# A fused last layer in a one-core attention kernel: part of the output product made ahead, in two other stages

## The chip, the cores and the metric

The kernel runs on one core of one Trainium2 chip. The metric is the device time of one execution in microseconds (us). Its engines here: TensorE (PE; PEld is its weight load), VectorE (DVE), ScalarE (ACT), GpSimd (POOL) and SyncE (SP), which issues DMAs only.

## The reference

x has 128 sequences of 32 rows and 256 features; everything is fp32.

```
x = x + einsum('bct,bcd->bdt', x, w0[subject])        # L0, 32x32 mixing of the rows, by sequence
x = x + einsum('bct,bcd->bdt', x, w1[condition])      # L1, the same
# L2: attention. q (8 heads of 32), k, v (4 heads) = projections of x; rms norm and rope on q, k;
#     the 32 new k, v rows are written into a paged cache (16 positions a block), a window of 128
#     positions is attended; o @ Wo.T is added
x2 = x + L2(x)
# L3: adapters by sequence
out = x2 + x2 @ W.T + scale[a] * (x2 @ A[a].T) @ B[a].T
```

## The kernel before

**Layout.** A tile is four sequences, 128 rows of x; there are 32 tiles, 16 pairs of tiles, and 64 couples (two sequences each, so two couples in a tile). A group is 8 sequences, two tiles, four couples. The stages:

Index and mixing stage, to about 50 us: which cache blocks a window needs, the row and window indices, and the 32x32 mixing matrices of L0 and L1 for all tiles (`mixT`).

Tile stage, about 50 to 157 us. A loop over pairs (`part2`). TensorE: `xT` of the even tile (L1006, x mixed and transposed), `qkv` (L1015, 512 columns), two `qT` transposes of the pair before (L1022), `xT` and `qkv` of the odd tile. ScalarE: squares (L534), a copy of v (L538), x2T out of PSUM (`xT_out`, L524), `keep_x`, a second copy of it to `xres` (L528), square roots, and the copy of v to `stage`. VectorE: sums of squares, norm, rope, `finish` (L759). GpSimd scatters the new k and v of each tile to `new_scratch` in DRAM (L433). `turn_indices` (L994, L999), on whose result VectorE waits before its first sum, stands behind the first two pairs on TensorE. qkv uses four PSUM banks (`psQKV`). After the `xres` copy this tensor holds x2's part before attention, which only the last layer reads.

Gap. When all scatters have landed, GpSimd fetches the patched blocks of groups 0 and 1 (`from_patched`, L446). VectorE makes masks meanwhile (L872 to L881) and adds the identity to W (`w3_plus_one`, L884), so that out = x2 (W + 1) + adapter. TensorE has nothing to do.

Attention stage, from 180 us. For each group GpSimd gathers the cache blocks (`fetch`, L439) and then the patched ones; SP writes the values to DRAM (`values_out`, L331) and reads them back transposed (`values_in`, L343, L345); they are in the list of SP in this order, with the output stores of two tiles (`store`, L324) between `values_out` and `values_in`. TensorE transposes keys four times a group (`unit`, L1071; L1188 for group 0), in the first two periods of the group before. There is a period for each couple c. TensorE's order in it: scores of c+1 (mask L1084, then L1089), values of c-1 (L1128), a unit, [odd: `adapter`, L1146], the transposes of c's probabilities (L1108, L1113), a unit, then [even: `project`, L1139; odd: `final`, L1152 and L1153] of the last tile. ScalarE: [even: `y_out`, L634], `heads_out` (L626), exponentials of c+1 in two halves (L610) with a unit's copy between and one at the end (L601), `probT_out` (L619). VectorE: maxima of c+1 (L890), [odd: `adapt_in`, L916], the copy of the probabilities (L907), reciprocal and scaling of c+1 (L896, L900), [even: `add3`, L911, between its halves]. Every engine works strictly through its own list; scores of c+2 wait until all exponentials of c+1 have read the four score banks (`expd`). Periods 0 to 7 and the last 8 are written out, the others are a loop of 8.

**The last layer** of a tile in the order of its data: `project` (o Wo, transposed, into bank `psZ`), `add3` (x3T = x2T + that), `adapter` (A x3T), `adapt_in` (times the adapter mask and scale, `xam`), `final` (x3 (W + 1) + xam B), `y_out` (PSUM to one of two buffers `ys`, after waiting for the buffer's store of two tiles ago), `store`. `project` of the next tile waits until `y_out` has emptied psZ.

## Time and profile before

| | us |
|---|---|
| runs | 495.17, 490.85, 505.08; median 495.17 |
| the profiled execution | 493.59 |
| its span, first to last instruction | 491.8 |
| PE busy (share) | 381.8 (78%) |
| DVE busy | 345.4 (70%) |
| ACT busy | 264.4 (54%) |
| POOL busy | 107.7 (22%) |
| mean granted TensorE clock | 0.906 |

The profile is one execution. Its times are from the start of the span; the ends of matmuls are modelled, and "[0.71 <-ACT ...]" behind an instruction is the idle time of its engine before it and what ended it. "issue" is time in which the engine waited for nothing that the profile shows. Each fp32 product of the program shows as two instructions (each L1015 below is four for two products).

### The profile page before, as it was taken

To read this page: it belongs to the slowest core of one execution; us is meant where nothing else is said; L and a number is where in the kernel's file an instruction comes from. 1 tells how busy PE (TensorE), PEld (TensorE's weight loads), DVE (VectorE), ACT (ScalarE), POOL (GpSimd) and SP (SyncE) were. 2 spreads that over 40 slices of the span, in tenths; PEclk is the share of its full clock that TensorE was granted. 3 is DMA by queue.
4 is the path that set the end of the run, shared out by engine and by line. 5 is a ranking of instruction groups with operands and counts; after the bars stand their busy time and mean duration, and the time that the engine had idled before them with its cause. 6 is when DMAs were issued, how large, how long until landed. Compare 5 with 4: busy or idle time off the path is not lost.

```text
span 491.8 us, 16903 instructions
## 1 busy us (share of the span) xinstructions
PE 381.8 (78%) x6190; PEld 283.1 (58%) x6190; DVE 345.4 (70%) x1017; ACT 264.4 (54%) x977; POOL 107.7 (22%) x178
## 2 busy tenths in 40 slices
PE   1753788888885027888798899999699999899996
PEld 0333534444442025676676777777577777777785
DVE  6995189999999515747666777777567677777782
ACT  3303556666664015646465766676456666766662
POOL 5300043333334700221112112111211212111000
PEclk9855789999998555989989999999989999999999
DMA  3999123222202266888887777967977666976200
GB/s 111 354 409 412 49 69 107 73 79 72 78 35 81 61 140 175 150 188 178 172 183 180 155 177 167 145 156 160 204 192 160 159 175 149 181 182 147 73 23 24
DMA packets 68867, 73.58 MB, mean 150 GB/s; under 512 B 18190, under 2 KB 65326, under 8 KB 66528
## 3 DMA queue, kind: packets, MB, share of 16 engines
q1 hardware_dynamic: 61968, 39.38, 33.5%
q0 software_dynamic: 6864, 33.72, 24.9%
q8 instruction: 23, 0.38, 0.3%
q14 instruction: 12, 0.10, 0.1%
HBM read 70.83 MB, written 26.21 MB: 197 GB/s over the span
## 4 chain that ended last, share of the span: by engine, by line
PE 48%; DMA 19%; ACT 12%; issue 11%; DVE 7%; SPq 1%; DVEq 1%; ACTq 0%; POOL 0%; POOLq 0%
ACT rope L610 6%; PE probT_bank L1128 6%; DMA kvbuf<-new_scratch,winidx 6%; PE out_bank L1152 5%; PE score_banks L1015 5%; PE score_banks L1089 5%; PE probT_bank L1015 4%; DMA value_scratch<-kvbuf 4%; PE keys_bank L1071 3%; PE score_banks L1084 3%; ACT window L601 3%; PE score_banks L1006 3%; DMA window<-value_scratch 3%; PE out_bank L1139 3%; DMA out<-early 3%
## 5 line engine op out<-in xcount | busy, mean ns | idle before, releaser
L610 ACT ACTIVATE rope<-score_banks,negm 128x176 f32<-128x176 f32 x256 | 101.8, 413 | 4.5 <-DVE negm L890 4.5
L890 DVE TENSOR_REDUCE negm<-score_banks 128x2 f32<-128x352 f32 x128 | 61.1, 519 | 34.6 <-PE score_banks L1089 34.1
L900 DVE TENSOR_SCALAR rope<-rope,rinv 128x176 f32<-128x176 f32 x256 | 70.9, 319 | 4.6
L626 ACT COPY early<-probT_bank 128x128 f32<-128x128 f32 x64 | 17.0, 266 | 88.6 <-PE probT_bank L1128 88.6
L433 POOL DMA_INDIRECT new_scratch<-stage,rowidx x32 | 36.5, 1139 | 106.7 <-DVE stage L759 101.7
L907 DVE COPY rope<-probT_bank 128x512 f32<-128x512 f32 x64 | 44.3, 692 | 18.0 <-PE probT_bank L1108 14.3
L610 ACT ACTIVATION_READ_ACCUMULATOR rope<-score_banks,negm 128x1 f32 x256 | 54.2, 212 | 0.0
L1128 PE MATMUL probT_bank<-rope,window 128*32 128x64 f32 x2048 | 43.7, 226 | 5.5 <-issue 4.7
L601 ACT COPY window<-keys_bank 128x352 f32<-128x352 f32 x60 | 46.8, 780 | 1.5 <-PE keys_bank L1071 1.5
L1071 PE MATMUL keys_bank<-ident,kvbuf 88*128 88x88 f32 x240 | 32.5, 260 | 16.3 <-ACT window L601 14.3
L1128 PEld LDWEIGHTS probT_bank<-rope,window 128*32 128x32 f32 x2048 | 32.8, 112 | 17.7 <-issue 17.7
L446 POOL DMA_INDIRECT kvbuf<-new_scratch,winidx x16 | 17.1, 1070 | 115.0 <-DMA kvbuf<-in_kv,winidx 112.2
L1108 PE MATMUL probT_bank<-ident,rope 128*128 128x128 f32 x256 | 40.8, 283 | 0.1
L1089 PE MATMUL score_banks<-window,rope 32*64 32x48 f32 (+2 forms) x1536 | 39.8, 292 | 0.0
L1084 PE MATMUL score_banks<-maskB,mask 96*128 96x176 bf16 x256 | 31.7, 248 | 7.8 <-ACT rope L610 6.9
L439 POOL DMA_INDIRECT kvbuf<-in_kv,winidx x16 | 17.4, 1087 | 92.0 <-PE keys_bank L1071 70.2
L1071 PEld LDWEIGHTS keys_bank<-ident,kvbuf 88*128 88x128 f32 x240 | 22.0, 145 | 26.6 <-ACT window L601 21.5
L1006 PE MATMUL score_banks<-kvbuf,work 128*128 (+1 forms) x128 | 22.1, 302 | 19.1 <-ACT x2T L524 16.6
L1139 PE MATMUL out_bank<-early,wts 128*128 128x128 f32 x256 | 36.3, 287 | 0.4 <-ACT early L626 0.4
L1006 PEld LDWEIGHTS score_banks<-kvbuf,work 128*128 128x128 f32 x128 | 18.3, 206 | 31.5 <-issue 28.9
L1152 PE MATMUL out_bank<-wts,early 128*128 128x256 f32 x128 | 34.9, 396 | 0.4 <-DVE early L916 0.4
L1139 PEld LDWEIGHTS out_bank<-early,wts 128*128 128x128 f32 x256 | 32.6, 200 | 0.6 <-ACT early L626 0.5
(184 smaller groups left out, 734.6 us busy)
## 6 DMA issues: line engine op xcount, KB each, us to landing
value_scratch<-kvbuf SPq DMA_DIRECT2D x16, 704.0 KB
window<-value_scratch SPq DMA_DIRECT2D x16, 512.0 KB, 11.7
work<-in_x SPq DMA_DIRECT2D x16, 256.0 KB, 2.7
new_scratch<-window SPq DMA_DIRECT2D x2, 2048.0 KB, 12.1
out<-early SPq DMA_DIRECT2D x32, 128.0 KB, 7.1
window<-value_scratch SPq DMA_DIRECT2D x32, 96.0 KB, 8.8
new_scratch<-kvbuf SPq DMA_DIRECT2D x1, 2048.0 KB, 13.4
wts<-in_weights SPq DMA_DIRECT2D x1, 1280.0 KB, 8.6
```

The source lines that it names most:

```text
L601: a.copy(kT[:, par, :, 4 * u:4 * u + 4].rearrange("p r o -> p o r"), psK[:, 0:4 * GR].rearrange("p (o r) -> p o r", o=4)).then_inc(s["unit ...
L610: ins = a.activation(prob[:, par, P_AT[h]:P_AT[h] + KEYS], psS[:, h, 0:KEYS], ACT.Exp, bias=negm[:, par, h:h + 1], accum_out=sums[:, par, ...
L890: v.tensor_reduce(negm[:, par, 2 * half:2 * half + 2], psS[:, 2 * half:2 * half + 2, 0:KEYS], axis=AX_X, op=ALU.max, negate=True).then_inc ...
L900: ins = v.tensor_scalar(prob[:, par, at], prob[:, par, at], rinv[:, par, h:h + 1], None, ALU.mult)
L907: v.tensor_copy(probT[:, par, 0:512], psP[0][:, :]).then_inc(s["pte0"], 1)
L1006: ins = t_.matmul(psT[j][:, P * c:P * c + P], xin[:, slot, P * c:P * c + P], mixT[:, bass.ds(n, 1), :].rearrange("p o d -> p (o d)"), star ...
L1071: ins = t_.transpose(psK[:, o * GR:(o + 1) * GR], kvbuf[0:GR, par, KV * (4 * u + o):KV * (4 * u + o) + P], ident[0:GR, 0:GR])
L1084: t_.matmul(psS[:, g_, 0:KEYS], mask4[:, tile, k % 2, :], maskB[:, g_ % 2].rearrange("p o i -> p (o i)"), start=True, stop=True, skip_grou ...
L1089: return t_.matmul(psS[64 * b:64 * b + 64, g_, n:n + BLOCK * blocks], qs[HD * g_:HD * g_ + HD, tile, P * (k % 2) + 64 * b:P * (k % 2) + 64 ...
L1128: ins = t_.matmul(headsT[HD * g_:HD * g_ + HD, 64 * b:64 * b + 64], vnat[:, (k // CPG) % 2, 2 * (k % CPG) + b, h, V_AT[g_]:V_AT[g_] + HD], ...
L1139: ins = t_.matmul(psZ[:, P * f:P * f + P], woT[:, u, P * f:P * f + P], oT[:, u, :], start=(u == 0), stop=(u == 1))
L1152: t_.matmul(psZ[:, 0:256], x3T[:, P * f:P * f + P], w3T[:, f, :], start=(f == 0), stop=False)
```

## The change

o Wo (W + 1) is linear, so the last layer splits: out = x2 (W + 1) + o [Wo (W + 1)] + (x2 A' + o [Wo A']) masked, times B. Wo (W + 1) and Wo A' are made once on TensorE in the gap (`fused`) and kept in `wo` and `woA`. x2's part of both (`x2_parts`: two products of 256 columns, two of 128) is made for even tiles in the tile stage, after the first qkv of a pair, into bank `psX`, and for odd tiles in the gap, into the four score banks in turn; ScalarE copies it over `xres` and into `xa2` (`x2_out`). So `keep_x` stays for odd tiles only; psX takes a bank from qkv, which now has two and waits for the norm and the v copy of the tile two back (it was four back). In the attention stage `project` gives o's two parts, `adapter` and `add3` are gone, `final` has the product with B alone, `y_out` moves to VectorE in even periods (ahead of the probabilities' copy) and adds `xres`, and `adapt_in` becomes an add of `xa2` and a separate mask step behind the copy. There are four buffers `ys`; SP's list has `values_in` ahead of the stores. `turn_indices` and `w3_plus_one` stand earlier. VectorE's loop has one more round of 8 periods written out. The semaphores and the closing waits follow.

```diff
@@ -139,11 +139,14 @@
         ident = sb("ident", [P, P])
-        work2 = sb("work2", [P, 3072])
+        work = sb("work", [P, 6144])
+        e1, work2 = work[:, 0:3072], work[:, 3072:]
+        xa2 = [work[:, a:a + TILES // 2 * P].rearrange("p (t n) -> p t n", n=P) for a in (3072, 1024)]
...
         w_at = [sum(W_PARTS[:k]) for k in range(len(W_PARTS))]
-        wqkvT, woT, w3T, laT = (wts[:, a:a + n].rearrange("p (c n) -> p c n", c=2) for a, n in zip(w_at[:4], W_PARTS))
+        wqkvT, wo, w3T, laT = (wts[:, a:a + n].rearrange("p (c n) -> p c n", c=2) for a, n in zip(w_at[:4], W_PARTS))
         lbT = wts[:, w_at[4]:]
+        woA = sb("adapted_wo", [P, 2, P])
...
@@ -251,11 +254,9 @@
         rinv = sb("rinv", [P, 2, KVH])
-        e1 = early[:].rearrange("p a b n -> p (a b n)")
-        oT = e1[:, 256:512].rearrange("p (u n) -> p u n", u=2)
-        x3T = e1[:, 512:768]
-        xam = e1[:, 768:896]
-        ys = e1[:, 896:1408].rearrange("p (a n) -> p a n", a=2)
+        oT = e1[:, 0:256].rearrange("p (u n) -> p u n", u=2)
+        xam = e1[:, 256:384]
+        ys = work2[:, 2048:3072].rearrange("p (a n) -> p a n", a=4)
@@ -264,10 +265,11 @@
-        psT, psQKV, psQT = [psS[:, 2], psS[:, 3]], psP + [psS[:, 0], psS[:, 1]], [psK, psZ]
+        psT, psQKV, psQT = [psS[:, 2], psS[:, 3]], psP + psP, [psK, psZ]
+        psX = psS[:, 1]
...
         all_entries = psZ[:, 0:ENT]
-        turned_rows, turned_wins = psS[:, 0, 0:ROWS], psS[:, 1, 0:2 * GROUPS]
+        turned_rows, turned_wins = psS[:, 0, 0:ROWS], psS[:, 0, ROWS:ROWS + 2 * GROUPS]
...
@@ -348,10 +350,10 @@
                 values_out(grp, par)
+                values_in(grp, par, False)
                 if not (isinstance(grp, int) and grp == 2):
-                    store(grp * 2 - 5, 1)
-                store(grp * 2 - 4, 0)
-                values_in(grp, par, False)
+                    store(grp * 2 - 5, 3 - 2 * par)
+                store(grp * 2 - 4, 2 * par)
...
@@ -523,6 +525,11 @@
+            def x2_out(p, n, bank, home):
+                act.wait_ge(s["x2_made"], p + 1)
+                a.copy(xres[:, bass.ds(n, 1), :].rearrange("p t f -> p (t f)"), bank[:, 0:256])
+                a.copy(home.rearrange("p o n -> p (o n)"), bank[:, 256:384]).then_inc(s["x2_kept"], 1)
...
@@ -568,13 +575,15 @@
                 if s1:
+                    wait_from(act, s["x2_made"], i + 2)
...
                 if s1:
-                    for j in range(2):
-                        keep_x(i * 2 + 4 + j, j)
+                    keep_x(i * 2 + 5, 1)
+                if s2:
+                    x2_out(i + 1, i * 2 + 2, psX, xa2[0][:, bass.ds(i + 1, 1), :])
@@ -626,13 +635,6 @@
-            def y_out(m, par):
-
-                act.wait_ge(s["l3"], m + 1)
-                if not (isinstance(m, int) and m < 2):
-                    act.wait_ge(s_out[par], (m - par) * 8)
-                a.copy(ys[:, par, :], psZ[:, 0:256]).then_inc(s["y"], 1)
...
@@ -640,8 +642,6 @@
                 units = k % CPG < 2 and not (known and group >= GROUPS)
-                if par == 0 and not (known and m < 2):
-                    y_out(m - 2, (k // 2) % 2)
@@ -653,6 +653,13 @@
+
+            act.wait_ge(s["fused"], 2)
+            for u in range(2):
+                a.copy(woA[:, u, :], psP[u][:, 256:384])
+                a.copy(wo[:, u, :], psP[u][:, 0:256]).then_inc(s["fused_kept"], 1)
+            for p in range(TILES // 2):
+                x2_out(PAIRS + p, 2 * p + 1, psS[:, p % 4], xa2[1][:, p:p + 1, :])
...
@@ -852,6 +857,11 @@
             v.tensor_copy(winidx[:].rearrange("p k g -> p (k g)"), turned_wins[0:GR]).then_inc(s["winidx"], 1)
+            dve.wait_ge(s["ld_w"], 16)
+            for c in range(2):
+                ins = v.tensor_tensor(w3T[:, c, P * c:P * c + P], w3T[:, c, P * c:P * c + P], ident[:], ALU.add)
+            ins.then_inc(s["w3_plus_one"], 1)
...
@@ -879,10 +889,6 @@
             ch.mark(v.tensor_scalar(admask[:], ad_f[:], pf[:, 2:3], pf[:, 3:4], ALU.is_equal, ALU.mult))
-            dve.wait_ge(s["ld_w"], 16)
-            for c in range(2):
-                ins = v.tensor_tensor(w3T[:, c, P * c:P * c + P], w3T[:, c, P * c:P * c + P], ident[:], ALU.add)
-            ins.then_inc(s["w3_plus_one"], 1)
@@ -906,15 +912,22 @@
-            def add3(m):
+            def y_out(m, q):
+                dve.wait_ge(s["l3"], m + 1)
+                if not (isinstance(m, int) and m < 4):
+                    dve.wait_ge(s_out[q], (m - q) * 4)
+                v.tensor_tensor(ys[:, q, :], xres[:, bass.ds(m, 1), :].rearrange("p o f -> p (o f)"), psZ[:, 0:256],
+                                ALU.add).then_inc(s["y"], 1)
+
+            def adapt_in(m, odd, at):
                 dve.wait_ge(s["wo"], m + 1)
-                v.tensor_tensor(x3T, xres[:, bass.ds(m, 1), :].rearrange("p o f -> p (o f)"), psZ[:, 0:256],
-                                ALU.add).then_inc(s["x3"], 1)
-
-            def adapt_in(m):
-                dve.wait_ge(s["xa"], m + 1)
-                v.tensor_tensor(xam.rearrange("p (b t) -> p b t", b=SPT),
-                                psZ[:, 256:256 + P].rearrange("p (b t) -> p b t", b=SPT),
+                wait_from(dve, s["l3"], m)
+                v.tensor_tensor(xam, psZ[:, 256:256 + P], xa2[odd][:, bass.ds(at, 1), :].rearrange("p o n -> p (o n)"),
+                                ALU.add).then_inc(s["xa_part"], 1)
+
+            def adapt_mask(m):
+                dve.wait_ge(s["xa_part"], m + 1)
+                v.tensor_tensor(xam.rearrange("p (b t) -> p b t", b=SPT), xam.rearrange("p (b t) -> p b t", b=SPT),
@@ -927,17 +940,18 @@
                 if par == 1 and not (known and m < 1):
-                    adapt_in(m - 1)
+                    adapt_in(m - 1, (k // 2 - 1) % 2, o * 2 + (k // 2 - 1) // 2)
+                if par == 0 and not (known and m < 2):
+                    y_out(m - 2, (k // 2 + 2) % 4)
                 probT_out(c, par)
+                if par == 1 and not (known and m < 1):
+                    adapt_mask(m - 1)
                 if not last:
-                    normalise(c + 1, 1 - par, 0)
-                if par == 0 and not (known and m < 1):
-                    add3(m - 1)
-                if not last:
-                    normalise(c + 1, 1 - par, 1)
+                    for half in range(2):
+                        normalise(c + 1, 1 - par, half)
             dve.wait_ge(s["qte"], TILES)
-            dve.wait_ge(s["xcopy"], TILES)
+            dve.wait_ge(s["xcopy"], PAIRS)
@@ -947,15 +961,18 @@
                 normalise(0, 0, half)
-            for k in range(8):
-                period(0, k)
-            with dve.Fori(1, COUPLES // 8 - 1) as o:
+            for o in range(2):
+                for k in range(8):
+                    period(o, k)
+            with dve.Fori(2, COUPLES // 8 - 1) as o:
...
                 period(COUPLES // 8 - 1, k)
-            add3(TILES - 1)
-            adapt_in(TILES - 1)
+            y_out(TILES - 2, 2)
+            adapt_in(TILES - 1, 1, PAIRS - 1)
+            adapt_mask(TILES - 1)
+            y_out(TILES - 1, 3)
@@ -1009,8 +1026,8 @@
                 pe.wait_ge(s["xte"], n + 1)
-                wait_from(pe, s["norm"], n - 3)
-                wait_from(pe, s["vcopy"], n - 3)
+                wait_from(pe, s["norm"], n - 1)
+                wait_from(pe, s["vcopy"], n - 1)
@@ -1022,6 +1039,13 @@
+            def x2_parts(xt, bank):
+                for f in range(2):
+                    t_.matmul(bank[:, 0:256], xt[f], w3T[:, f, :], start=(f == 0), stop=(f == 1))
+                for f in range(2):
+                    ins = t_.matmul(bank[:, 256:384], laT[:, f, :], xt[f], start=(f == 0), stop=(f == 1))
+                ins.then_inc(s["x2_made"], 1)
...
@@ -1030,6 +1054,8 @@
                     qkv(i * 2 + 2, 2 - slot)
+                    wait_from(pe, s["x2_kept"], i + 1)
+                    x2_parts([x2T[:, 0, f, :] for f in range(2)], psX)
@@ -1039,11 +1065,11 @@
             pe.wait_ge(s["mixT"], 2)
+            turn_indices()
...
             pe.wait_ge(s["ld_w"], 16)
+            pe.wait_ge(s["w3_plus_one"], 1)
             part2(-1, 2, True, True, False)
-            turn_indices()
-            pe.wait_ge(s["winidx"], 1)
@@ -1057,7 +1083,18 @@
             pe.wait_ge(s["vcopy"], TILES)
-            pe.wait_ge(s["w3_plus_one"], 1)
+            pe.wait_ge(s["xcopy"], PAIRS)
+
+            for u in range(2):
+                for at, n, w in ((0, 256, w3T), (256, P, laT)):
+                    for f in range(2):
+                        ins = t_.matmul(psP[u][:, at:at + n], wo[:, f, P * u:P * u + P], w[:, f, :], start=(f == 0), stop=(f == 1))
+                ins.then_inc(s["fused"], 1)
+            pe.wait_ge(s["x2_kept"], PAIRS)
+            for p in range(TILES // 2):
+                if p >= 4:
+                    pe.wait_ge(s["x2_kept"], PAIRS + p - 3)
+                x2_parts([xres[:, 2 * p + 1, P * f:P * f + P] for f in range(2)], psS[:, p % 4])
@@ -1134,23 +1171,15 @@
                 wait_from(pe, s["y"], m)
-                for f in range(2):
-                    for u in range(2):
-                        ins = t_.matmul(psZ[:, P * f:P * f + P], woT[:, u, P * f:P * f + P], oT[:, u, :],
-                                        start=(u == 0), stop=(u == 1))
+                for u in range(2):
+                    t_.matmul(psZ[:, 256:256 + P], woA[:, u, :], oT[:, u, :], start=(u == 0), stop=(u == 1))
+                for u in range(2):
+                    ins = t_.matmul(psZ[:, 0:256], oT[:, u, :], wo[:, u, :], start=(u == 0), stop=False, skip_group_check=True)
...
-
-            def adapter(m):
-                pe.wait_ge(s["x3"], m + 1)
-                for f in range(2):
-                    ins = t_.matmul(psZ[:, 256:256 + P], laT[:, f, :], x3T[:, P * f:P * f + P], start=(f == 0), stop=(f == 1))
-                ins.then_inc(s["xa"], 1)
...
                 pe.wait_ge(s["xam"], m + 1)
-                for f in range(2):
-                    t_.matmul(psZ[:, 0:256], x3T[:, P * f:P * f + P], w3T[:, f, :], start=(f == 0), stop=False)
-                t_.matmul(psZ[:, 0:256], xam, lbT, start=False, stop=True).then_inc(s["l3"], 1)
+                t_.matmul(psZ[:, 0:256], xam, lbT, start=False, stop=True, skip_group_check=True).then_inc(s["l3"], 1)
@@ -1165,8 +1194,6 @@
                     unit(group, (k // CPG + 1) % 2, 2 * (k % CPG))
-                if par == 1 and not (known and m < 1):
-                    adapter(m - 1)
@@ -1189,6 +1216,8 @@
             pe.wait_ge(s["first_units"], 2)
+            pe.wait_ge(s["fused_kept"], 2)
+            pe.wait_ge(s["x2_kept"], TILES)
...
@@ -1220,7 +1248,7 @@
     wqkv = _np.concatenate([wq, t("Wk"), wv], axis=0)
-    wo = t("Wo").reshape(FEAT, KVH, 2, HD).transpose(1, 3, 2, 0).reshape(P, -1)
+    wo = t("Wo").reshape(2, P, KVH, 2, HD).transpose(1, 0, 3, 2, 4).reshape(P, -1)
...
```

## Rows read from the trace of the kernel before

**Rows 1.** Windows: stretch and its length, busy time of engines, granted clock, DMA.
```profile
180.00:200.00 20.00, 16.00 (x224) 12.14 (x225) 10.58 (x30) 11.24 (x35) 2.88 (x4) 0.56 0.58 152
400.00:450.00 50.00, 45.87 (x909) 37.59 (x902) 36.19 (x112) 32.60 (x129) 8.69 (x16) 1.00 0.76 170
```

**Rows 2.** Chain of waits in the tile stage: start, length, what.
```profile
123.07 0.71 PE score_banks L1006 x4
...
126.38 1.73 PE score_banks L1015 x4
...
129.22 0.71 PE score_banks L1006 x4
```

**Rows 3.** Chain of waits in the attention stage.
```profile
420.47 0.94 PE out_bank L1139 x8
...
425.20 0.90 PE out_bank L1152 x4
```

**Rows 4.** Chain of waits at the start of the tile stage.
```profile
55.95 1.72 PE probT_bank L1015 x4
...
61.07 3.33 PE score_banks L1015 x4
```

**Rows 5.** Timeline of TensorE, end of the gap: start, length, instruction, idle before.
```profile
180.11 0.82 PE L1188 MATMUL keys_bank<-ident,kvbuf 88*128 88x88 f32 x4 [21.39 <-DMA kvbuf<-new_scratch,winidx]
```

**Rows 6.** Timeline of TensorE, first groups.
```profile
209.39 0.49 PE L1071 MATMUL keys_bank<-ident,kvbuf 88*128 88x88 f32 x4 [2.08 <-DMA kvbuf<-new_scratch,winidx]
...
215.38 0.65 PE L1128 MATMUL probT_bank<-rope,window 128*32 128x64 f32 x32 [0.79 <-DMA window<-value_scratch]
...
229.28 0.64 PE L1128 MATMUL probT_bank<-rope,window 128*32 128x64 f32 x27 [0.98 <-issue]
```

**Rows 7.** Timeline of TensorE, one group and its neighbours.
```profile
412.43 0.47 PE L1084 MATMUL score_banks<-maskB,mask 96*128 96x176 bf16 x4 [0.36 <-ACT rope L610]
...
416.55 0.47 PE L1084 MATMUL score_banks<-maskB,mask 96*128 96x176 bf16 x4
...
419.94 0.52 PE L1071 MATMUL keys_bank<-ident,kvbuf 88*128 88x88 f32 x4 [0.71 <-ACT window L601]
...
421.23 0.47 PE L1084 MATMUL score_banks<-maskB,mask 96*128 96x176 bf16 x4
...
426.37 0.47 PE L1084 MATMUL score_banks<-maskB,mask 96*128 96x176 bf16 x4
...
430.08 0.48 PE L1084 MATMUL score_banks<-maskB,mask 96*128 96x176 bf16 x4 [0.31 <-ACT rope L610]
```

**Rows 8.** Groups of VectorE's instructions, and two of its timeline.
```profile
L872 DVE TENSOR_TENSOR start_bc<-len_f,rem_bc 128x128 f32<-128x128 f32 x1 | 0.3, 284 | 0.0
...
417.66 0.96 DVE L890 TENSOR_REDUCE negm<-score_banks 128x2 f32<-128x352 f32 x2 [0.44 <-PE score_banks L1089]
...
421.56 0.42 DVE L911 TENSOR_TENSOR early<-xres,out_bank 128x256 f32<-128x256 f32 x1 [1.09 <-PE out_bank L1139]
```

**Rows 9.** Timeline of ScalarE and TensorE around 355 us.
```profile
355.18 0.37 ACT L634 COPY early<-out_bank 128x256 f32<-128x256 f32 x1 [5.46 <-DMA out<-early]
...
358.02 0.80 PE L1084 MATMUL score_banks<-maskB,mask 96*128 96x176 bf16 x4
...
363.60 0.47 PE L1084 MATMUL score_banks<-maskB,mask 96*128 96x176 bf16 x4
```

**Rows 10.** Timeline of SP's DMA issues for one group: start, time to issue.
```profile
413.09 0.94 SPq L331 DMA_DIRECT2D value_scratch<-kvbuf  x1
414.34 3.41 SPq L324 DMA_DIRECT2D out<-early  x2
421.48 0.41 SPq L343 DMA_DIRECT2D window<-value_scratch  x1
422.07 3.99 SPq L345 DMA_DIRECT2D window<-value_scratch  x2
```

**Rows 11.** Timeline of TensorE, the last tile.
```profile
484.84 1.16 PE L1139 MATMUL out_bank<-early,wts 128*128 128x128 f32 x8 [0.38 <-ACT early L626]
```

21 lines of the change are left out of this document (9 added, 12 removed).

## The prediction

> **What bounds the kernel now.** I read the stages first (windows), since the change touches three of them. The tile stage (about 60 to 152 us) I read in the chain of waits [rows 2]: a pair of tiles takes 6.15 us from one row at L1006 to the next. TensorE works 5.04 us of that without a break, until the second L1015 ends at 128.11; the other 1.11 us is ScalarE's squares, values and x2T copy. Whatever TensorE gets more there lengthens each pair. Then comes a gap: TensorE stands 21.39 us, from 158.72 on, until group 0's patched cache block lands and L1188 begins at 180.11 [rows 5]. From there 64 couples follow. Their start is paced by transfers: TensorE waits for group 2's keys until 209.39 and for group 1's values until 215.38 [rows 6]. Later the couples pace themselves; TensorE is busy 45.87 of 50 us, VectorE 36.19, ScalarE 32.60 [rows 1]. A row at L1084 opens each period [rows 7]: 4.12 us from the first row to the second (a fourth period of its group), then 4.68, 5.14 and 3.71 (first, second, third): 17.65 us for a group of two tiles. Two ends are seen in them. Before 412.43 and 430.08 TensorE waits for ScalarE's exponentials, so a third period is a loop of scores, maxima and exponentials. The other three have no wait before L1084: TensorE's own queue ends last, and in the first two of a group that queue stands once in the middle, at the second keys transpose, for ScalarE's copy (0.71 us at 419.94).
>
> **The profiled execution** took 493.59 us with 491.8 of span; the 1.8 around it I keep. The median of the runs is 1.6 above it. I sum against 493.59.
>
> **Tile stage.** Each pair gets x2_parts between the first qkv and qT: two products of 256 columns and two of 128. The trace gives each fp32 product as two instructions. Four of 256 columns take 0.90 us in the chain, eight of 128 take 0.94, so four take 0.47 [rows 3]: 1.37 us. From L1015 (1.73 for four of 512 columns, so 0.86 for 256) it is 1.33. I take 1.35. It lies wholly on the path, since ScalarE's squares of the second tile wait for a qkv that starts so much later. Fifteen pairs count (the part of pair -1 falls into the start, below): 15 x 1.35 = 20.2 us. ScalarE loses keep_x of the even tile and gets two copies, the larger like L634's 0.37 [rows 9]; while TensorE works its 5 us, ScalarE has air for them, and they end before the next x2_parts, so that the single bank psX costs nothing. The stricter wait of qkv (two banks, not four) asks for the norm of the tile two back, a pair earlier on VectorE; it gets 1.35 us more air by the longer pair. At the start the index turn (0.7 us) now stands ahead of the first xT and pair -1 has its x2 part: about 0.6 later together, because the turn stood until now in a stretch where TensorE waited anyway. In return the hole before 60.38 shrinks; the qkv at 61.07 ran at the low clock, 3.33 us against 1.72 at 55.95 [rows 4]. If the clock holds, 1.6 comes back; I take half. Stage: **+20.0** (18.5 to 21.5). POOL's scatters follow VectorE, which follows this path, so the last scatter, group 0's block and all its followers shift by as much.
>
> A rule of the Trainium skill would make this half as dear: "TensorE: Matmul & The Clock Gate", section Back-to-back issue gap, gives N / 2.4 + 2.5 ns for a matmul at full clock, 109 ns for 256 columns. By it the part costs some 0.66 us and the stage +10. The rows show 0.43 us for an instruction of 512 fp32 columns and 0.22 for 256 [rows 2, 3], twice the page's figure; I go by the rows.
>
> **Gap,** in before's time (all of it 20.0 later). TensorE is free at about 159.1. The fused weights are four products of 256 and four of 128 columns, 2.7 us, the sixteen odd parts 21.6. It begins at the low clock; the dense start at 50 us had L1015 back at 1.72 by 55.95 [rows 4], some 5 us at half speed, so 2.4 more. ScalarE's copies lie beside, with four banks. That ends at 185.8, 5.7 us after the block's landing, plus 0.5 if code is late. But TensorE then starts warm (the clock granted in 180 to 200 was 0.56 [rows 1]), and the group's transfers go on without it. Walking on from there (transposes 3.3, periods 3.6, 4.2, 4.2, 3.8, 3.6) the sixth scores begin at 208.5; before it was 205.74. Group 2's keys land at 209.4 and group 1's values at 215.4 as before [rows 6], and the overrun drowns in these waits, up to some 1.4 us more of it. I take **+0.5** (0 to +5). The moved w3_plus_one sits in idle time of VectorE.
>
> The Trainium skill, "Runtime: NRT & Kernel Launch", section Instruction fetch mechanics, says that code is streamed in blocks of 256 instructions, mostly hidden. In the trace TensorE stands 0.98 us inside one product loop at 229.28 with nothing to wait for [rows 6]. The gap's 288 instructions would cross one or two blocks: by the page nothing, by that row 1 to 2 us, which is inside the range above.
>
> **Couples, period by period.** Of a tile's projection (0.94), adapter (0.47 to 0.6) and final (0.90 + 0.45 [rows 3]) there remain 0.47 + 0.90 = 1.37 in the even period and 0.45 in the odd one, 0.9 less. But not evenly:
> First of a group: the second keys transpose still starts 3.39 after the period (419.94, it waits for ScalarE), takes 0.52, then 1.40 instead of 0.94: 4.68 becomes 5.14.
> Second: the same transpose at +3.36, 0.52, final 0.45, and the exponentials end about there: 5.14 becomes 4.20.
> Third: the loop's 3.71, but project now waits for VectorE's y_out, which stands behind the maxima. These start 1.11 after the period and last 0.96, y_out 0.42 like L911 [rows 8], so project starts at 2.55 and ends the period at 3.80.
> Fourth: 4.12 was TensorE's queue; with adapter gone and the final short it is the loop, 0.1 below the third's because ScalarE has no keys copy left over: 3.60.
> Sum 16.74 against 17.65, 0.91 a group. From 215 us on 14.5 groups: **-13.2** (-8 to -17). VectorE's mask step is nearest to L872, 128x128 in SBUF, 0.284 [rows 8].
>
> **Stores.** At 355.18 ScalarE's y_out had stood 5.46 us for an output store (two buffers), and heads_out behind it, on which TensorE waits. Some 4.4 of it were lost to TensorE, and the next period, partly at the low clock, took 5.58 (358.02 to 363.60) instead of 4.12 [rows 9]: 5.9 us. With four buffers the wait looks two tiles further back, 17 us, and the store is issued some 9 us later than now. **-5.9** (to 0). Values first: values_in was issued at 421.48, when values_out of 413.09 had landed [rows 10]; the stores were issued inside that wait, so the order by itself gains nothing. It moves their issue behind values_in on SP, ahead of the next values_out. SP was done with values_in at 426.1 and had some 5 us left there.
>
> **Tail.** From 484.84 [rows 11] to the last store's issue at about 489.6 stand project 1.2, add3 0.45, adapter 0.75, adapt_in 0.35, final 1.6 and y_out 0.4. Then they are project 1.6, adapt_in 0.35, mask 0.3, final 0.5 and y_out 0.45: 1.5 less. The last values, behind the shorter final of tile 30, start 0.5 sooner: **-2.0** (-1 to -2.5).
>
> **Sum:** 493.6 + 20.0 + 0.5 - 13.2 - 5.9 - 2.0 = **493.0 us**. With the bounds taken partly together its own range is 486 to 501.
>
> **Rivals.**
> A, all of TensorE's removed work returns: 0.92 x 29 tiles = 27 us instead of 13: 479. For it: 45.87 of 50 us busy [rows 1]. Against: the waits at 419.94, 412.43 and 430.08 [rows 7], which no removed product shortens. 0.12.
> B, slower: VectorE takes TensorE's place. It is busy 36.19 of 50 us [rows 1], 3.19 a period of 4.41, and 3.32 with half a mask step; add3 goes, y_out comes. The shortest periods above are 3.60 and 3.80, and its steps stand in order, so each waits for the transposes, too. If these waits add 0.3 to 0.5, project (behind y_out) and final (behind the mask) come late, each period grows 0.22, a group takes 17.6 and the steady gain is gone: 493.0 + 13.2 = 506. It decides once the mean period is above 4.4. 0.14.
> C, the gap runs cold: x2_parts at 2.7 us each end at 207, 21 us later than above, and 18 of it show: 511. For it, the clock of 0.56 in 180 to 200 [rows 1]; against, that stretch has short bursts, and 50 to 56 us recovered [rows 4]. 0.05. (The Trainium skill's clock page, section Loop structure matters more than you think, says that dense products keep the high clock; by it C is out.)
> D, the buffers don't do what they say: a late store or late values stop an engine as at 355: 499. 0.08, beside 0.61 for the forecast.
>
> **How the numbers follow.** Two per cent (9.9 us) is about what a measurement of this kernel can tell from no change, with runs from 490.85 to 505.08. The range 483 to 506 leaves out A, most of C and the upper half of B, about 0.2. Faster than 485.3: A and a little of the forecast, 0.15. Slower than 505.1: C, over half of B and a little more, 0.16. Within: 0.69.
>
> **What would show it.** In the trace after: rows at L1006 7.5 us apart in the tile stage; L1188 at about 206, long after its block's landing near 200; periods of 5.1, 4.2, 3.8 and 3.6; no engine waiting for a store. VectorE with no idle before the maxima would be B, x2_parts of over 2 us in the gap C. I would be wrong most if a period ends on something that before's waits hid: a late block of keys, or SP, whose round of values_out, wait, values_in and two stores comes to about 15 of 16.7 us.

## The result and the profile after

The changed kernel took **502.61 us** (median of 4 runs, 499.58 to 505.22) where the kernel before took 495.04 (median of 4, 490.85 to 505.08). Executions of one kernel come in a faster and a slower state, and medians here are over all runs, ratios over those of the faster state alone. The ratio is 1.023, 95% interval 1.016 to 1.030: slower by 2.3% (1.6 to 3.0). The forecast was 493.0, no change. The profiled execution after took 500.77, with 498.9 of span against 491.8: 7.1 us more.

The page after: engines (us busy, share, instructions), then the median time to landing of SP's transfers.

```profile
span 498.9 us, 17056 instructions
...
PE 400.6 (80%) x6206; PEld 290.9 (58%) x6206; DVE 348.2 (70%) x1049; ACT 264.5 (53%) x997; POOL 107.8 (22%) x178
...
window<-value_scratch SPq DMA_DIRECT2D x16, 512.0 KB, 12.8
...
out<-work SPq DMA_DIRECT2D x32, 128.0 KB, 7.5
window<-value_scratch SPq DMA_DIRECT2D x32, 96.0 KB, 10.4
```

TensorE has 18.8 us more to do. On the page of the kernel before, the value windows landed after 11.7 and 8.8 us. Line numbers moved: L1006 is now L1023, L1015 is L1032, L1071 is L1108, L1084 is L1121; x2's part is L1044 and L1046, project L1175 and L1177, the final product L1182, y_out L919, the mask L930.

Windows of the kernel after, as [rows 1]; the stretch 200 to 220 holds its first couples:

```profile
180.00:200.00 20.00, 20.00 (x117) 18.30 (x116) 4.48 (x6) 7.48 (x28) 7.55 (x7) 0.93 0.41 92
200.00:220.00 20.00, 15.89 (x186) 12.82 (x184) 8.35 (x23) 12.03 (x41) 2.85 (x4) 0.75 0.62 160
400.00:450.00 50.00, 41.94 (x858) 31.66 (x860) 35.67 (x116) 29.48 (x121) 10.26 (x17) 1.00 0.83 173
```

In 400 to 450 us TensorE works less than before (41.94 us, not 45.87), while the DMA share rose from 0.76 to 0.83: of the work that was taken away a part came back as waiting.

The chain of waits in the tile stage, one pair, as [rows 2]:

```profile
98.64 0.71 PE score_banks L1023 x4
99.34 1.72 PE probT_bank L1032 x4
101.06 0.86 PE score_banks L1044 x4
101.93 0.45 PE score_banks L1046 x4
...
106.09 0.71 PE score_banks L1023 x4
```

A pair takes 7.45 us instead of 6.15, and the 1.31 us of the two new rows is the difference.

TensorE's timeline in the attention stage: the first scores, one group, then late values, as [rows 6, 7]:

```profile
207.01 0.48 PE L1121 MATMUL score_banks<-maskB,mask 96*128 96x176 bf16 x4 [0.84 <-DVE window L958]
...
338.04 0.47 PE L1121 MATMUL score_banks<-maskB,mask 96*128 96x176 bf16 x4
...
341.44 0.52 PE L1108 MATMUL keys_bank<-ident,kvbuf 88*128 88x88 f32 x4 [0.71 <-ACT window L610]
341.80 0.64 PE L1175 MATMUL out_bank<-work,adapted_wo 128*128 128x128 f32 x4
...
343.14 0.47 PE L1121 MATMUL score_banks<-maskB,mask 96*128 96x176 bf16 x4
...
347.43 0.47 PE L1121 MATMUL score_banks<-maskB,mask 96*128 96x176 bf16 x4
...
350.06 0.68 PE L1175 MATMUL out_bank<-work,adapted_wo 128*128 128x128 f32 x4 [0.18 <-DVE work L919]
...
351.45 0.47 PE L1121 MATMUL score_banks<-maskB,mask 96*128 96x176 bf16 x4
...
354.59 0.70 PE L1182 MATMUL out_bank<-wts,work 128*128 128x256 f32 x2 [0.61 <-DVE work L930]
355.13 0.47 PE L1121 MATMUL score_banks<-maskB,mask 96*128 96x176 bf16 x4
...
414.87 0.65 PE L1165 MATMUL probT_bank<-rope,window 128*32 128x64 f32 x32 [1.54 <-DMA window<-value_scratch]
```

The periods of a group are 5.10, 4.29, 4.02 and 3.68: 17.09 against 17.65. Project now waits for VectorE's y_out and the final product for its mask. At 414.87 the values are late, and that period took 5.92 instead of 4.29. No engine waits for a result store any more (compare [rows 9]).

For every kernel below I read the same three marks off TensorE's timeline: the first scores row (start of attention), the eighth (by then the first groups' transfers are in), and the last, the 64th. For the kernel before they lie at 184.12, 219.54 and 476.79; after, at 207.01, 239.38 and 485.38. So the change cost 19.84 us up to the eighth couple, gave 11.25 from there to the 64th (257.25 to 246.00) and 1.49 in the tail (15.01 to 13.52): 7.1 together, the whole difference of the spans. "8th to 64th" is this second distance; it holds 14 groups.

### The profile page after: what moved, and what is told of

It is laid out like the page before. It is cut to its first block, busy times and chain, and to the rows that moved or that the text cites. A ratio compares the mean times of both kernels' runs of the same rounds, so it can differ in the third digit from the quotient of the medians.

```text
span 498.9 us, 17056 instructions
## 1 busy us (share of the span) xinstructions
PE 400.6 (80%) x6206; PEld 290.9 (58%) x6206; DVE 348.2 (70%) x1049; ACT 264.5 (53%) x997; POOL 107.8 (22%) x178
## 3 DMA queue, kind: packets, MB, share of 16 engines
q1 hardware_dynamic: 61968, 39.38, 34.4%
q0 software_dynamic: 6864, 33.72, 25.2%
## 4 chain that ended last, share of the span: by engine, by line
PE 62%; DMA 10%; issue 10%; ACT 9%; DVE 8%; ACTq 1%; SPq 0%; DVEq 0%; POOLq 0%
PE probT_bank L1032 11%; PE score_banks L1126 6%; PE score_banks L1044 6%; PE probT_bank L1165 5%; PE out_bank L1177 5%; PE score_banks L1023 4%; PE keys_bank L1108 4%; PE score_banks L1121 3%; PE out_bank L1182 3%; PE out_bank L1175 3%; ACT window L610 3%; PE score_banks L1046 3%; ACT rope L619 3%; DMA kvbuf<-new_scratch,winidx 3%; DMA kvbuf<-in_kv,winidx 3%
## 5 line engine op out<-in xcount | busy, mean ns | idle before, releaser
L635 ACT COPY work<-probT_bank 128x128 f32<-128x128 f32 x64 | 17.1, 266 | 110.4 <-PE probT_bank L1165 110.4
L906 DVE TENSOR_SCALAR rope<-rope,rinv 128x176 f32<-128x176 f32 x256 | 69.8, 315 | 4.6
L1032 PE MATMUL probT_bank<-wts,x2T 128*128 128x512 f32 x128 | 61.5, 603 | 1.0 <-ACT x2T L526 1.0
L913 DVE COPY rope<-probT_bank 128x512 f32<-128x512 f32 x64 | 44.2, 690 | 19.1 <-PE probT_bank L1145 18.5
L1108 PE MATMUL keys_bank<-ident,kvbuf 88*128 88x88 f32 x240 | 33.5, 266 | 19.9 <-ACT window L610 19.4
L1145 PE MATMUL probT_bank<-ident,rope 128*128 128x128 f32 x256 | 42.4, 290 | 0.0
L1108 PEld LDWEIGHTS keys_bank<-ident,kvbuf 88*128 88x128 f32 x240 | 22.8, 149 | 30.3 <-ACT window L610 26.4
L541 ACT ACTIVATE work<-probT_bank 128x384 f32<-128x384 f32 x32 | 15.7, 491 | 39.8 <-PE probT_bank L1032 39.8
L1023 PE MATMUL score_banks<-kvbuf,work 128*128 (+1 forms) x128 | 21.9, 300 | 15.7 <-ACT x2T L526 15.7
L1023 PEld LDWEIGHTS score_banks<-kvbuf,work 128*128 128x128 f32 x128 | 17.9, 204 | 27.1 <-issue 27.1
L1121 PE MATMUL score_banks<-maskB,mask 96*128 96x176 bf16 x256 | 31.0, 244 | 3.2 <-ACT rope L619 2.4
L1177 PE MATMUL out_bank<-wts,work 128*128 128x256 f32 x128 | 33.1, 380 | 0.0
## 6 DMA issues: line engine op xcount, KB each, us to landing
window<-value_scratch SPq DMA_DIRECT2D x16, 512.0 KB, 12.8
window<-value_scratch SPq DMA_DIRECT2D x32, 96.0 KB, 10.4
```

Source lines behind the costliest of these rows:

```text
L906: ins = v.tensor_scalar(prob[:, par, at], prob[:, par, at], rinv[:, par, h:h + 1], None, ALU.mult)
L913: v.tensor_copy(probT[:, par, 0:512], psP[0][:, :]).then_inc(s["pte0"], 1)
L1023: ins = t_.matmul(psT[j][:, P * c:P * c + P], xin[:, slot, P * c:P * c + P], mixT[:, bass.ds(n, 1), :].rearrange("p o d -> p (o d)"), star ...
L1032: ins = t_.matmul(psQKV[j][:, :], x2T[:, j % 2, c, :], wqkvT[:, c, :], start=(c == 0), stop=(c == 1))
L1108: ins = t_.transpose(psK[:, o * GR:(o + 1) * GR], kvbuf[0:GR, par, KV * (4 * u + o):KV * (4 * u + o) + P], ident[0:GR, 0:GR])
L1121: t_.matmul(psS[:, g_, 0:KEYS], mask4[:, tile, k % 2, :], maskB[:, g_ % 2].rearrange("p o i -> p (o i)"), start=True, stop=True, skip_grou ...
```

## Experiments

Sixteen kernels. "Group" is the length of four periods where nothing is late, "8th to 64th" the distance of those marks, both from the profiled execution. "Ratio" is to the kernel before, run beside it on the same chip (its medians there: 495.6 for the first four, 493.8 for the second, 497.9 for the third, 499.2 for the last four). The profiled executions of h and i took 506.1 and 503.4 us, 3.2 and 6.9 above their medians, so their marks carry less weight.

| kernel | median us | ratio, 95% | group | 1st / 8th scores | 8th to 64th |
|---|---|---|---|---|---|
| before | 495.04 | | 17.65 | 184.1 / 219.5 | 257.3 |
| after | 502.61 | 1.023 [1.016, 1.030] | 17.09 | 207.0 / 239.4 | 246.0 |
| a_no_tile_parts | 481.12 | 0.978 [0.968, 0.987] | 17.09 | 183.8 / 214.4 | 248.3 |
| b_stores_first | 497.55 | 1.022 [1.012, 1.032] | 17.09 | 205.3 / 239.6 | 241.1 |
| c_before_four_buffers | 491.51 | 1.007 [0.996, 1.017] | 17.65 | 185.4 / 221.1 | 251.8 |
| d_odd_behind | 479.73 | 0.984 [0.980, 0.988] | 17.09 | 184.3 / 218.8 | 245.0 |
| e_project_first | 497.88 | 1.009 [1.002, 1.015] | 16.23 | 206.2 / 237.0 | 243.8 |
| h_no_gap_parts | 502.95 | 1.019 [0.989, 1.049] | 17.09 | 202.0 / 238.1 | 252.6 |
| i_adds_first | 496.58 | 1.012 [0.990, 1.034] | 16.71 | 205.4 / 240.5 | 248.6 |
| g_all (d + e + i) | 479.18 | 0.976 [0.956, 0.995] | 15.79 | 187.3 / 219.3 | 246.4 |
| k_all_stores (g + b) | 476.51 | 0.965 [0.953, 0.976] | 15.79 | 185.9 / 221.0 | 241.3 |
| r_all_no_stores | 476.00 | 0.959 [0.949, 0.968] | 15.79 | 184.5 / 219.8 | 242.8 |
| n_before_one_gather | 476.42 | 0.966 [0.957, 0.975] | 17.65 | 185.1 / 216.3 | 244.4 |
| m_after_one_gather | 489.67 | 0.994 [0.990, 0.998] | 17.09 | 206.0 / 236.2 | 237.3 |
| p_no_gap_one_gather | 486.63 | 0.979 [0.968, 0.991] | 17.09 | 203.2 / 235.6 | 237.2 |
| q_adds_first_one_gather | 482.30 | 0.970 [0.960, 0.980] | 16.71 | 207.3 / 238.3 | 231.4 |
| o_behind_one_gather | 468.27 | 0.942 [0.933, 0.951] | 17.09 | 188.3 / 218.2 | 237.2 |
| l_all_one_gather | 449.26 | 0.911 [0.903, 0.920] | 15.79 | 187.8 / 217.4 | 219.3 |

**What the tile stage costs.** a_no_tile_parts leaves the even tiles' part out.

```diff
-                    wait_from(pe, s["x2_kept"], i + 1)
-                    x2_parts([x2T[:, 0, f, :] for f in range(2)], psX)
```

> The changed kernel without the even tiles' x2 products in the tile stage (left out altogether, so the even tiles' results lack x2's part; ScalarE keeps x2T of both tiles as before). If these products lie wholly on TensorE's path (15 times 1.31 us), a pair takes 6.15 us again and the time falls from 502.6 by 19 to 20, to about 483. If the tile stage has other new costs (two qkv banks instead of four), a pair stays above 6.15 and the time above 486. If the loss is in the couples and not here, the time stays near 500.

Measured 481.12, first scores at 183.8 instead of 207.0, a pair 6.14 us (rows at L1021 at 100.76 and 106.90), as the first theory said. d_odd_behind keeps all the work and moves it: the odd tile's part behind the second qkv, the even tiles' in the gap.

```diff
-                    wait_from(pe, s["x2_kept"], i + 1)
-                    x2_parts([x2T[:, 0, f, :] for f in range(2)], psX)
...
                     qkv(i * 2 + 3, 3 - slot)
+                    wait_from(pe, s["x2_kept"], i + 1)
+                    x2_parts([x2T[:, 1, f, :] for f in range(2)], psX)
```

> The changed kernel with the odd tiles' x2 products in the tile stage, behind the second qkv, in place of the even ones' behind the first (the even ones go to the gap, as many as before). TensorE stood 1.11 us there in each pair for ScalarE. If place and not amount is what costs, a pair takes 6.3 to 6.5 instead of 7.45 us and the time falls by 14 to 17, to 486 to 489. If ScalarE's path grows in its stead (xT_out of the odd tile now waits for the products), a pair takes about 7 and the time is near 496. If the amount alone counts, 502.

Measured 479.73, 22.9 us less than the changed kernel by the medians of the two series and 21.6 by the spans (477.3 against 498.9), and better than the 486 to 489 that I gave it. Its chain of waits, one pair:

```profile
101.78 1.72 PE probT_bank L1032 x4
...
103.94 0.45 PE score_banks L1023 x4
104.38 1.72 PE probT_bank L1032 x4
106.10 0.86 PE score_banks L1044 x4
106.97 0.44 PE score_banks L1046 x4
107.41 0.52 PE score_banks L1023 x4
107.93 1.29 PE probT_bank L1032 x3
```

The pair is 6.15 us (101.78 to 107.93), as in the kernel before, with the same four products in it: 1.11 us of their 1.30 fill the time that TensorE stood there for ScalarE, and the first product of the next pair (L1023 at 107.41), 0.71 us long after a stand [rows 2], takes 0.52 without one. In 60 to 180 us TensorE is busy 115.45 of 120, against 98.21 after; that counts the products of the gap, which begin sooner here. So the 20 us are a matter of place.

**The order on SP, and the buffers.** b_stores_first puts the stores of a group ahead of its values_in again; c_before_four_buffers is the kernel before with four result buffers.

```diff
 # b
-                values_in(grp, par, False)
                 if not (isinstance(grp, int) and grp == 2):
                     store(grp * 2 - 5, 3 - 2 * par)
                 store(grp * 2 - 4, 2 * par)
+                values_in(grp, par, False)
 # c
-                    act.wait_ge(s_out[par], (m - par) * 8)
+                    act.wait_ge(s_out[par], (m - par) * 4)
```

> The changed kernel with the two stores ahead of values_in on SP again, four buffers kept. If the late values at the second periods of three groups (0.9, 1.6 and 0.8 us over 4.29) come from stores sent right behind values_in and moving beside it, values_in lands sooner (median 12.8 now, 11.7 before) and the time falls by 3 to 4, to about 499. If the order is indifferent and the values are late because the couples run faster, nothing changes (502 to 503).

> The kernel before with nothing but four result buffers (ScalarE's y_out as it was). The prediction booked 5.9 us for the stall at 355. If that stall is in every execution, the time falls from 495.0 to about 489. If it is an accident of some executions, the median moves by 0 to 3 and the longest runs come down. If buffers don't matter, no change and ScalarE's waits on stores stay.

b: the median is 5 us lower than after's, but of another series; by the ratios, 1.022 and 1.023, there is no difference. Its windows landed after 12.0 and 9.6 us instead of 12.8 and 10.4, and TensorE waited 0.9 us for values instead of 3.0. That points one way, but is not shown by the times. c: the median is 4 us below before's, its longest run 493.9 against 499.5, yet the ratio 1.007 [0.996, 1.017] shows no gain: three executions of before beside it took 486.9 to 489.3 us without the edit. The two profiles do differ by the size of the wait at 355 us [rows 9]: "8th to 64th" is 5.4 us shorter in c, where no engine waits for a store. One profile of before can't tell whether that wait is part of every execution.

**Shorter couples.** e_project_first puts project ahead of the second keys transpose in the even period; i_adds_first puts VectorE's pieces of the last layer ahead of the maxima; g_all has both and d's place for x2's part.

```diff
 # e, in period of TensorE
                 probs_T(c, par)
+                if par == 0 and not (known and m < 1):
+                    project(m - 1)
                 if units:
                     unit(group, (k // CPG + 1) % 2, 2 * (k % CPG) + 1)
 # i, in period of VectorE: moved ahead of maxes(c + 1, 1 - par, half)
+                if par == 1 and not (known and m < 1):
+                    adapt_in(m - 1, (k // 2 - 1) % 2, o * 2 + (k // 2 - 1) // 2)
+                    adapt_mask(m - 1)
+                if par == 0 and not (known and m < 2):
+                    y_out(m - 2, (k // 2 + 2) % 4)
```

> The changed kernel with one order turned in the even couples: the three products with oT (project) ahead of the second four transposes of a unit, instead of behind them. My theory: in the first couple of a group project, whose inputs are ready at about +3.5 us, stands behind the second unit, which waits 0.70 us for ScalarE's copy of the first; turned, the period of 5.10 falls to about 4.4, 0.7 us in each of 14.5 groups, so about 10 us less: 492.5 us (490 to 495), with the other three periods of a group as they are. Rival 1: the maxima and exponentials set this couple anyway, the period stays at 4.9 or more: 500 us. Rival 2: the gathers set the pace (the DMA engines are busy 0.83 of the time): couples get shorter and the time comes back as waits for value windows or gathered rows at the start of a group: 499 us or more.

> The changed kernel with VectorE's pieces of the last layer (the final addition; the addition and the mask for the adapter) ahead of the maxima of the next couple instead of behind them, where VectorE idles 0.4 to 1.0 us for the scores. My theory: what the third couple of a group (4.02 us) loses against 3.68 is project's wait for the final addition, which stands behind the maxima; it goes to 3.7 to 3.8, the second one to 4.2, the others stay (the first is set by the second unit, the fourth by ScalarE's exponentials): 0.3 to 0.4 us in each of 14.5 groups, 5 us less: 497.5 us (496 to 499.5). Rival: VectorE is the bound of each couple, and any order costs the same: 502.6 us. Second rival: the maxima come later by these pieces and each couple grows by 0.2 to 0.4 us: 506 us or more.

> Three edits together: odd tiles' x2 products behind the second qkv in the tile stage (479.7 us alone, before), project ahead of the second unit in even couples, and VectorE's pieces of the last layer ahead of the maxima. My theory: they add, 479.7 less 10 less 5 is 464.7 us (462 to 469), with a group of four couples at about 16.1 us. Rival: the gathers and the value windows set a floor on a group near 17 us, then 476 us or more. Half way (470 to 475): the couples shrink but the waits at group starts grow.

The periods did what was expected, e's first 4.23 instead of 5.10, i's third 3.71 instead of 4.02 (its second stayed at 4.29), g's group 15.79. The times did so only for i: its 496.58 lies in the expected 496 to 499.5, with an interval of 2% to either side. e should have come to 492.5 and took 497.88. g_all should have come to 464.7 and took 479.18, as d alone. Its timeline of TensorE shows where the time went:

```profile
260.56 0.91 PE L1125 MATMUL score_banks<-window,rope 32*64 32x48 f32 x12 [3.71 <-issue]
...
319.87 0.82 PE L1107 MATMUL keys_bank<-ident,kvbuf 88*128 88x88 f32 x4 [1.01 <-DMA kvbuf<-new_scratch,winidx]
...
359.87 0.65 PE L1164 MATMUL probT_bank<-rope,window 128*32 128x64 f32 x32 [1.53 <-DMA window<-value_scratch]
...
392.84 0.49 PE L1107 MATMUL keys_bank<-ident,kvbuf 88*128 88x88 f32 x4 [2.00 <-DMA kvbuf<-new_scratch,winidx]
```

and its chain of waits has nothing of length in it but DMA from 310 to 346 us:

```profile
310.54 11.56 DMA kvbuf<-in_kv,winidx
...
322.94 13.22 DMA kvbuf<-new_scratch,winidx
...
336.42 9.37 DMA value_scratch<-kvbuf
```

The three links (the two gathers of a group, and the writing out of its values) and what lies between take 35.3 us (310.54 to 345.79), after which the buffer may be filled again. There are two buffers, so a group costs about 17.6 here. Divide "8th to 64th" by its 14 groups: 17.2 to 18.4 us in every kernel with both gathers, whether its couples need 15.8 or 17.65. The 35.3 is one round in one profile, and the quotients also hold the waits of other kinds, so 17.6 is a size and not an exact floor (b and k come to 17.2).

**The gap.** h_no_gap_parts leaves out the products of the gap.

```diff
-            for p in range(TILES // 2):
-                if p >= 4:
-                    pe.wait_ge(s["x2_kept"], PAIRS + p - 3)
-                x2_parts([xres[:, 2 * p + 1, P * f:P * f + P] for f in range(2)], psS[:, p % 4])
```

> The changed kernel without the 16 groups of x2 products of the odd tiles in the gap (96 matmuls, 21 us of TensorE; their results are left out of the output). My theory: the gap is filled by transfers in any case; the first scores come up to 3 us earlier, and the first groups' gathered rows take that back by the eighth couple: 502.6 less 0 to 1 us. Rival: the parts in the gap do lie on the path by the 3 us by which the first scores are later than the tile stage alone explains: 499.5 us. Second rival: the clock falls when the gap has no matmuls (it was 0.52 to 0.75 in the first 20 us of attention otherwise) and that costs some 2 us: 504 to 505.

Measured 502.95, with an interval of 3% to either side: it tells nothing about 1 to 3 us. Its marks say more: the first scores come 5.0 us sooner than after's, the eighth 1.2.

**The best order, and the transfers quiet.** k_all_stores is g_all with b's edit. The other three are g_all, after and before without the second gather of each group from the third on:

```diff
-            from_patched(2, 0)
...
-                from_patched(grp, grp % 2)
...
-                    pe.wait_ge(s_patched[par], (grp - par) * 8 + 16)
+                    pe.wait_ge(s_patched[par], 16)
```

> The three edits together (odd tiles' x2 products behind the second qkv, project ahead of the second unit, VectorE's pieces ahead of the maxima; 479.2 us) and, as a fourth, the two stores of a group ahead of its value windows again, as in the kernel before. My theory: in the three-edit kernel a group of couples takes 15.8 us where nothing is late, but 18.0 on the mean, since value windows and gathered rows land late; the windows are then better off behind the stores, whose transfers are over before them: 3 to 5 us less, 474 to 476 us. Rival: now that the couples are faster, windows issued later land later: 481 us or more.

> The three-edit kernel (479.2 us) without the second gather of each group from the third on (the 14 transfers of rows written in this call into the window buffers; so keys and values of the new blocks are left out from there). My theory: the chain of a buffer (11.8 us for the first gather, about 12 for the second, then the units, then the same buffer again) needs 33 to 35 us for two groups, the couples only 31.6; without the second gather the couples set the pace, the 16 us by which the five stretches of eight couples from 266 to 439 us exceed 31.6 each go, and the result is 463 us (458 to 466), groups at 15.8. Rival: the excess is late value windows or code loading, not the gathers: 472 us or more. Second rival: VectorE or ScalarE is the bound and no transfer matters: 479 us.

> The changed kernel (502.6 us) without the second gather of each group from the third on (new rows left out). My theory: its couples need 34.2 us for two groups, close to what the buffers' chain needs; only its late value windows (3.3 us in all) and a part of the stalls at the first loop's start go: 497 us (494 to 499.5), groups at 17.1. Rival: the transfers are not involved: 502.6 us. Other rival: the transfers hold this kernel up as much as the three-edit one, by 12 us or more: 490 us or less.

> The kernel before without the second gather of each group from the third on (new rows left out). My theory: its couples need 35.3 us for two groups, more than the chain of the buffers, so only the waits for a result buffer (5.5 us in the profiled run) and some of the stalls of the first loop go: 4 us less than before on this chip, 490 us (488 to 493); the gap between it and the changed kernel without the gather is then 7 us, as it is with it. Rival: transfers hold the kernel before up by more than the changed one: under 486 us.

k_all_stores came 0.5 us above its 474 to 476 and is the fastest complete kernel here, 3.5% faster than before; that the order of the stores gives its last 3 us is not shown (g_all's interval overlaps). The other three fell much further than my theory gave them: 449 instead of 463, 490 instead of 497, 476 instead of 490; for m and n the rival that gave more to the transfers came true. The kernel before had 12.9 us of waiting in it between the 8th and 64th scores, of which I had named only the 5.9 around 355 us. Periods of before and of after without the second gather:

```profile
325.78 0.47 PE L1082 MATMUL score_banks<-maskB,mask 96*128 96x176 bf16 x4 [0.35 <-ACT rope L608]
329.90 0.47 PE L1082 MATMUL score_banks<-maskB,mask 96*128 96x176 bf16 x4
334.58 0.47 PE L1082 MATMUL score_banks<-maskB,mask 96*128 96x176 bf16 x4
339.72 0.47 PE L1082 MATMUL score_banks<-maskB,mask 96*128 96x176 bf16 x4
343.43 0.47 PE L1082 MATMUL score_banks<-maskB,mask 96*128 96x176 bf16 x4 [0.31 <-ACT rope L608]
```

```profile
342.82 0.47 PE L1119 MATMUL score_banks<-maskB,mask 96*128 96x176 bf16 x4
346.50 0.47 PE L1119 MATMUL score_banks<-maskB,mask 96*128 96x176 bf16 x4
351.59 0.47 PE L1119 MATMUL score_banks<-maskB,mask 96*128 96x176 bf16 x4
355.89 0.47 PE L1119 MATMUL score_banks<-maskB,mask 96*128 96x176 bf16 x4
```

The steady periods are those of the full kernels to 0.02 us, and they stay so in every group, from the ninth couple on, but for a few that are up to 0.12 longer. What went are all the irregular ones, those of the first loop too. So the kernels with both gathers are paced by two things in turn: the couples' own pace, and a wait for transfers wherever these are behind.

**Each term alone.** o, p, q are m_after_one_gather with the edit of d, h and i; r_all_no_stores is g_all without the stores of results in the loop.

> The changed kernel with the odd tiles' x2 products behind the second qkv, and without the second gather of each group from the third on (new rows left out). Where the transfers are quiet each difference is one term. My theory: TensorE idles about 1.3 us in a pair behind the second qkv and none of the 15 pairs grows: 489.7 less 20 is 469.7 us (468 to 472), first scores at 186. Rival: products anywhere in the pair cost their time: 489 us.

> The changed kernel without the 16 groups of x2 products of the gap (left out of the output) and without the second gather of each group from the third on. My theory: the gathers of the first two groups cover the gap's products but for their last 3.5 to 4 us (in the run with both gathers the first scores came at 202.3 instead of 207.0); with nothing to take that back it stays: 489.7 less 4 is 485.7 us (485 to 487). Rival, that of the prediction: 0.5 us in the gap: 489.2 us. Second rival: the cold TensorE in an empty gap costs the first couples 2 us: 487.5 to 488.

> The changed kernel with VectorE's pieces of the last layer ahead of the maxima, and without the second gather of each group from the third on. My theory: a group takes 16.71 us instead of 17.10 (the value that the prediction gave: 16.74): 489.7 less 0.39 x 14.5 (5.7) is 484.0 us (483 to 485.5), and the distance to the kernel before under the same edit, 13.3 us, falls to 7.6. Rival: the transfers hid a cost of this order that shows when they are quiet: 488 us or more.

> The three-edit kernel (479.2 us) with both gathers, but without the stores of the results in the loop (28 of 32 tiles are never written out; 256 of about 3070 KB that a group moves) and without the waits for them. It tells a load from a chain. Theory of the load (each transfer lands later the more the others move, landing medians 12.5 us for windows against 4.4 us without the second gather): the landings get shorter by a tenth or more, and of the 30 us that the transfers cost here 6 to 12 go: 467 to 473 us. Theory of the chain (the second gather counts because it stands between the first and the units): stores are in no chain but the windows': 476 us or more.

o: 468.27, 21.4 less than m by the medians, as expected, and 18.1 by the spans; a pair takes 6.15 us, the first scores come at 188.3 and not at the expected 186.

p: 486.63, 3 us less by the medians and 0.7 by the spans (486.4 and 487.1); by the marks the first scores come 2.9 sooner, the eighth 0.6. My "nothing takes that back" was wrong. Three things in p's trace did: the first period took 4.03 instead of m's 3.40, with a granted clock of 0.50 in 200 to 210 us (m: 0.96); TensorE waited 0.62 for the first values (at 214.01), and stood 0.70 on "issue" (227.40). So the rival with the cold TensorE was right in part, by some 0.6 of its 2 us.

q: 482.30, 7.4 less than m by the medians, 4.8 by the spans; 8th to 64th fell from 237.3 to 231.4.

r: 476.00, 3 us less than g_all, just on the side that I had given to the chain; the 512 KB windows landed after 13.5 us in 260 to 430 us where g_all's landed after 13.1, the first gathers after 12.0 (11.6), the second ones after 12.0 (14.0). Its profile also has one wait of 8.03 us for a second gather that took 19.85 (302.37 to 322.21), more than g_all has at once. Fewer bytes outside the chain didn't shorten the windows' landings, but this is thin, and one removal can't tell load from chain for the second gather itself, which is both.

## Why the prediction was wrong

The forecast was 9.6 us low: it had the loss in the tile stage right and booked 6.2 us too much gain in the couples and up to 5.9 for a wait on stores. Against the profiled executions it said -0.6 and the spans gave +7.1. Term by term, with the quiet pair n and m beside it:

| term | forecast | profiles before, after | quiet pair n, m |
|---|---|---|---|
| tile stage and gap, to the 8th scores | +20.5 | +19.84 | +19.95 |
| couples | -13.2 | | -7.03 |
| stores | -5.9 | | |
| couples and transfer waits, 8th to 64th | -19.1 | -11.25 | -7.03 |
| tail | -2.0 | -1.49 | -1.42 |
| sum | -0.6 | +7.1 | +11.5 |

**Tile stage: right.** 1.31 us a pair against 1.35 forecast, on the path as said, and the price of an instruction by the rows (0.22 us for 256 columns), not the half of it by the Trainium skill's "TensorE: Matmul & The Clock Gate", section Back-to-back issue gap. What the prediction didn't ask is whether the part lay there of need.

**Gap: right.** First scores at 207.0 (by the forecast's steps 209.1: 185.8, 3.3 of transposes, 20.0 later), and the overrun drowned in the waits for the first groups' transfers: the 2.08 and 0.79 us that TensorE waited for them before [rows 6] are gone. Of the gap's parts 0.6 us is left at the eighth couple in p, 1.2 in h, against the +0.5 given. TensorE kept its high clock in them (0.93 granted in 180 to 200), so C is out.

**Couples: the step that failed.** The forecast group was 16.74, the measured one 17.09, and the term 7.0 instead of 13.2. Of the 6.2 between them 4.9 are 0.35 in each of 14 groups, and the largest piece, 0.22, is the third period (3.80 forecast, 4.02 measured). The prediction itself had project start 2.55 us after the period began; with the 1.40 that it gave project in the first period it ends at 3.95, not 3.80. The rest of that period is VectorE: y_out was done at 349.92 and project began at 350.06, 2.63 after the period:

```profile
349.51 0.41 DVE L919 TENSOR_TENSOR work<-xres,out_bank 128x256 f32<-128x256 f32 x1
```

The second period was 0.09 longer than forecast. There the prediction put the second keys transpose 3.36 us after the period, but on TensorE's timeline it stands at 3.45 before (424.68 less the 421.23 of [rows 7]) and at 3.46 after (346.60 less 343.14):

```profile
424.68 0.52 PE L1071 MATMUL keys_bank<-ident,kvbuf 88*128 88x88 f32 x4 [0.29 <-ACT window L601]
```

```profile
346.60 0.52 PE L1108 MATMUL keys_bank<-ident,kvbuf 88*128 88x88 f32 x4 [0.78 <-ACT window L610]
```

The fourth was 0.08 longer, where the final product waits for the mask (354.59), the first 0.04 shorter. The other 1.3 us are bookkeeping: 14.5 groups were booked and 14 lie between the marks (0.5), and at both ends of that stretch the periods are not the steady ones and fall by less; the last seven fell by 0.76 (28.95 in n, 28.19 in m), where 0.56 a group would give 0.98.
That the third and fourth periods were lost by VectorE's order, not its load, is shown by q: with its pieces ahead of the maxima they take 3.71 and 3.61, a group is 16.71, and 8th to 64th is 231.4, which is 12.9 less than n's 244.4. Nearly all of the 13.2 was to be had, by an order that the change doesn't have. Rival B named the right place (project behind y_out, final behind the mask) and gave it a price of 0.22 a period; it took 0.09 on the mean. Rival A (479) is out: the waits at the keys transpose (0.71 at 341.44) stayed, as argued against it.

**Stores: a wait of one execution, booked for all.** The transfer waits between the 8th and 64th scores were 257.25 - 244.36 = 12.9 us before and 246.00 - 237.33 = 8.7 after, so 4.2 came back where I wrote 5.9. The wait for a store is gone, and late values took a part of its place (3.0 us in three waits, one of them at 414.87). But I took one wait of the profiled execution as a part of the kernel, and c's ratio shows no gain from the buffers alone. Whether these 4.2 are in the timed runs is open: the ratio of the two kernels, 1.023, is 11.4 us of 495 (7.7 to 15.0 by its interval), as much as the quiet pair's spans differ by (11.5), while the medians differ by 7.6, like the spans of the two profiles.

**What I didn't see** is that for a part of the groups the transfers, not the couples, set the pace. The signs of it were in the trace of before: irregular periods, SP's round of some 15 of 16.7 us, a DMA share of 0.76. I named SP's round as what would make me wrong most. It cost little here, since the couples only came to 17.09 a group. In the profiles the transfers swallowed most of e's 12 us (0.86 in 14 groups): "8th to 64th" is 243.8 against after's 246.0, the median fell by 4.7. i's profile, of a long execution, shows 248.6 and so nothing of its 5 us, while its median fell by 6.0 with an interval of 2% to either side; that stays open.

What stays open besides: how far the second gather counts by its bytes and how far by its place in the chain, and whether SP's order is worth its 3 to 5 us.
